# Project stage of an adaptive-layernorm transformer block: token normalisation moved from VectorE to ScalarE, and two of eight subtractions of a half moved to GpSimd

## The reference, cut to what matters

```python
h = _layernorm(x, axis=-1) * (1 + ca) + sa          # (x - m) / sqrt(v + eps), then modulation
x = x + ga * attention(h)
h = _layernorm(x, axis=-1) * (1 + cb) + sb
x = x + gb * ffn(h)

# attention(x):
q = x @ W_q; k = x @ W_k; v = x @ W_v
latent_kv = (k + v) @ W_down_kv
k_rec = latent_kv @ W_up_k; v_rec = latent_kv @ W_up_v
scores = (q k_rec^T / sqrt(256)) * exp(-0.01 * |t - t'|)
out = softmax(scores) @ v_rec @ W_o
```

## Time and profile before

| what | value |
|---|---|
| median of 3 runs | 2593.89 us (2593.72 to 2594.16) |
| the profiled execution | 2596.16 us, of which the span of the trace is 2594.4 us |
| project stage, from the first projections to the last low part | about 36 to 341 us of the span |
| busy over the whole span | PE 93%, VectorE 80%, ScalarE 71%, GpSimd 50% |

### The profile page before, as it was taken

How to read it: one execution, slowest core, us unless ns; L and a number is a source line. 1 busy time by engine, 2 the same in 40 slices (tenths; PEclk the granted TensorE clock), 3 DMA queues, 4 the chain that set the end, 5 groups by cost and what they waited for, 6 DMA issues and landing times. The chain is left out here.

```text
span 2594.4 us, 41397 instructions
## 1 busy us (share of the span) xinstructions
PE 2425.1 (93%) x12710; PEld 1050.6 (40%) x12710; DVE 2068.6 (80%) x3812; ACT 1840.0 (71%) x4200; POOL 1289.9 (50%) x1107
## 2 busy tenths in 40 slices
PE   5878859999999999999999999999986999999998
PEld 2434312333333333333333333333223666666665
DVE  5888878888888888888888888888755878888885
ACT  3666615888888888888888888888843555555553
POOL 3666642534435344353453534534214777777774
PEclk9676757999999999999999999999976999999999
DMA  4777894755756657566574665755302111221110
GB/s 142 240 253 254 247 193 119 155 127 124 158 101 147 135 118 152 113 140 143 112 158 114 140 143 108 155 118 124 80 25 67 57 57 57 57 56 57 54 43 19
DMA packets 273773, 315.58 MB, mean 122 GB/s; under 512 B 38032, under 2 KB 182160, under 8 KB 273424
## 3 DMA queue, kind: packets, MB, share of 16 engines
q1 hardware_dynamic: 264336, 304.54, 49.2%
q10 hardware_dynamic: 9216, 8.39, 0.9%
HBM read 225.78 MB, written 85.46 MB: 120 GB/s over the span
## 5 line engine op out<-in xcount | busy, mean ns | idle before, releaser
L942 DVE CUSTOM_DVE_ANT_0 unread<-max_ps,toeplitz_sb 128x1024 bf16<-128x1024 f32 x1024 | 1215.7, 1222 | 248.9 <-PE max_ps L759 246.6
L871 ACT ACTIVATE probs<-score_ps 128x512 f32<-128x512 f32 (+3 forms) x2560 | 1015.3, 484 | 150.0 <-PE score_ps L788 75.5
L759 PE MATMUL max_ps<-k_low,q_low 96*128 96x512 bf16 x2048 | 718.0, 392 | 27.6 <-DVE ident_bf L933 17.9
L714 POOL TENSOR_TENSOR diag<-diag,diag_decay 128x512 f32<-128x512 f32 x240 | 305.5, 1273 | 811.7 <-ACT diag L880 807.2
L814 PE MATMUL pv_ps<-probs,v 128*32 128x512 f32 x4096 | 545.3, 605 | 1.7 <-ACT probs L900 0.7
L783 PE MATMUL score_ps<-q_up,k_up 99*128 99x512 bf16 (+3 forms) x1280 | 407.6, 319 | 13.9 <-ACT probs L871 12.4
L788 PE MATMUL score_ps<-q_low,k_low 99*128 99x512 bf16 (+3 forms) x1280 | 403.3, 317 | 3.6 <-ACT probs L871 3.0
L726 POOL TENSOR_TENSOR diag<-diag,shift 128x512 f32<-128x512 f32 x256 | 333.8, 1304 | 81.6 <-DVE diag L966 62.4
L1366 PE MATMUL gu_ps<-wgu_t,turned 128*128 128x512 f32 (+1 forms) x768 | 316.7, 562 | 0.8 <-DVE hid L1581 0.8
L759 PEld LDWEIGHTS max_ps<-k_low,q_low 96*128 96x128 bf16 x2048 | 197.0, 98 | 217.7 <-DVE row_max L942 107.5
L783 PEld LDWEIGHTS score_ps<-q_up,k_up 99*128 99x128 bf16 x1280 | 123.5, 97 | 378.3 <-ACT probs L871 201.4
(11 more groups left out here) (154 smaller groups left out, 2853.6 us busy)
## 6 DMA issues: line engine op xcount, KB each, us to landing
shift<-max_whole_dram SPq DMA_DIRECT2D x64, 1024.0 KB, 7.9
splits<-parts SPq DMA_DIRECT2D x128, 384.0 KB, 2.7
q_low<-splits SPq DMA_DIRECT2D x192, 128.0 KB, 7.3
k_low<-splits SPq DMA_DIRECT2D x192, 128.0 KB, 8.6
q_up<-splits SPq DMA_DIRECT2D x192, 128.0 KB, 11.6
k_up<-splits SPq DMA_DIRECT2D x192, 128.0 KB, 12.7
v_padded<-v_out SPq DMA_DIRECT2D x64, 256.0 KB, 3.7
v<-v_padded SPq DMA_DIRECT2D x32, 512.0 KB, 14.9
```

The source lines that it names most:

```text
L714: nc.gpsimd.tensor_tensor(diag[:, g % 2], diag[:, g % 2], diag_decay[:].unsqueeze(1).broadcast_to([P, UH, P]), ALU.mult).then_inc(diag_dec ...
L759: mm = pe.matmul(max_ps[:, i % 2, half * HALF:(half + 1) * HALF], low[0][u][0:KROWS, h, qb * P:(qb + 1) * P], low[1][u][0:KROWS, h, half * ...
L871: op = nc.scalar.activation(probs[:, g % PROBS, h, first:end], score_ps[:, at % RING, first:end], ACT.Exp)
L942: nc.vector.tensor_tensor_reduce(unread[:, i % 2, :], max_ps[:, i % 2, :], toeplitz[:, at:at + S], 1.0, -3.0e38, ALU.mult, ALU.max, row_ma ...
```

## The change

Normalisation goes to ScalarE as one scaled and shifted copy, x * rstd + (-mean * rstd). For that VectorE computes `minus_mean` (128x4) after `var_eps`, and GpSimd computes `offset` = `minus_mean` * `rstd` (128x4) after `rstd`. `var_ready` counts both VectorE operations, `rstd_ready` is now given by the `offset` product, and the power gives a new semaphore, `inverse_ready`, on which the product waits. `normalise(h + 1)` stands at the head of half h in ScalarE's program. VectorE no longer frees `x_in` (`x_free` is gone); SP waits for `xhat_ready` instead. Its place in SP's order is the same.

Of the eight subtractions `rest = full - high` of a half, those of blocks 0 and 4 go to GpSimd, each directly ahead of the low part of the same block; six stay on VectorE. The middle parts of blocks 0 and 4 (ScalarE) wait for GpSimd's new semaphore `pool_rest_ready`, and so does VectorE before it overwrites `full` 0 and 4 a half later.

```diff
+    POOL_RESTS = (0, 4)
         def load_x(b, hf):
             h = 2 * b + hf
-            sp.wait_ge(x_free, h + 1)
+            if h >= 2:
+                sp.wait_ge(xhat_ready, TH * (h - 1))
...
         def statistics(b, hf):
+            if h > 0:
+                dve.wait_ge(rstd_ready, h)
             for i in range(TH):
                 nc.vector.bn_aggr(mean_var[:, i, :], stats[:, i, :]).then_inc(aggr_done, 1)
             dve.wait_ge(aggr_done, TH * (h + 1))
             nc.vector.tensor_scalar(var_eps[:], mean_var[:, :, 1], EPS, None, ALU.add).then_inc(var_ready, 1)
-        def normalise(b, hf):
-            h = 2 * b + hf
-            dve.wait_ge(rstd_ready, h + 1)
-            for i in range(TH):
-                op = nc.vector.tensor_scalar(xhat[hf][:, i, :], x_in[hf][:, i, :], mean_var[:, i, 0:1],
-                                             rstd[:, i:i + 1], ALU.subtract, ALU.mult)
-                op.then_inc(xhat_ready, 1)
-            dve.wait_ge(xhat_ready, TH * (h + 1))
-            dve.sem_inc(x_free, 1)
+            nc.vector.tensor_scalar(minus_mean[:], mean_var[:, :, 0], -1.0, None, ALU.mult).then_inc(var_ready, 1)
...
             def scaled(n):
+                if n in POOL_RESTS and h > 0:
+                    dve.wait_ge(pool_rest_ready, len(POOL_RESTS) * (h - 1) + POOL_RESTS.index(n) + 1)
...
-                if n > 0:
+                if n > 0 and n - 1 not in POOL_RESTS:
                     without_high(n - 1)
...
         def inverse_std(h):
-            pool.wait_ge(var_ready, h + 1)
-            nc.gpsimd.tensor_tensor(rstd[:], var_eps[:], minus_half[:], ALU.pow).then_inc(rstd_ready, 1)
+            pool.wait_ge(var_ready, 2 * (h + 1))
+            if h > 0:
+                pool.wait_ge(xhat_ready, TH * h)
+            nc.gpsimd.tensor_tensor(rstd[:], var_eps[:], minus_half[:], ALU.pow).then_inc(inverse_ready, 1)
+            pool.wait_ge(inverse_ready, h + 1)
+            nc.gpsimd.tensor_tensor(offset[:], minus_mean[:], rstd[:], ALU.mult).then_inc(rstd_ready, 1)
 
         def low_parts(b, hf):
             for n in range(BLOCKS):
                 nb = BLOCKS * (2 * b + hf) + n
-                pool.wait_ge(rest_ready, nb + 1)
+                if n in POOL_RESTS:
+                    pool.wait_ge(high_ready, nb + 1)
+                    nc.gpsimd.tensor_tensor(rest[:, n % RING, :], full[:, n % RING, :], parts[:, n % RING, 0, :],
+                                            ALU.subtract).then_inc(pool_rest_ready, 1)
                 pool.wait_ge(middle_ready, nb + 1)
...
+        def normalise(b, hf):
+            h = 2 * b + hf
+            act.wait_ge(rstd_ready, h + 1)
+            for i in range(TH):
+                nc.scalar.activation(xhat[hf][:, i, :], x_in[hf][:, i, :], ACT.Identity, bias=offset[:, i:i + 1],
+                                     scale=rstd[:, i:i + 1]).then_inc(xhat_ready, 1)
...
         def middle(b, hf, n):
-            act.wait_ge(rest_ready, BLOCKS * (2 * b + hf) + n + 1)
+            h = 2 * b + hf
+            if n in POOL_RESTS:
+                act.wait_ge(pool_rest_ready, len(POOL_RESTS) * h + POOL_RESTS.index(n) + 1)
+            else:
+                others = [i for i in range(BLOCKS) if i not in POOL_RESTS]
+                act.wait_ge(rest_ready, len(others) * h + others.index(n) + 1)
```

More of the change, by code:

```diff
@@ L175, in project_stage @@
     rstd = sb("rstd", [P, TH], F32)
+    minus_mean = sb("minus_mean", [P, TH], F32)
+    offset = sb("offset", [P, TH], F32)
     h_t = [sb(f"h_t{i}", [P, DC, HALF], F32) for i in range(2)]
@@ L198, in project_stage @@
         sem("full_ready"), sem("high_ready"), sem("rest_ready"), sem("middle_ready"), sem("low_ready"))
-    x_free, lat_free, q_free, k_free = sem("x_free"), sem("lat_free"), sem("q_free"), sem("k_free")
+    lat_free, q_free, k_free = sem("lat_free"), sem("q_free"), sem("k_free")
+    inverse_ready, pool_rest_ready = sem("inverse_ready"), sem("pool_rest_ready")
     parts_free = [sem(f"parts_free{i}") for i in range(RING)]
@@ L258, in _ @@
     def _(dve):
-        dve.sem_inc(x_free, 2)
         dve.sem_inc(q_free, 1)
@@ L317, in steps @@
             for hf in range(2):
-                if later(b, hf, 1):
-                    normalise(*later(b, hf, 1))
                 splits(b, hf)
         statistics(0, 0)
-        normalise(0, 0)
         statistics(0, 1)
@@ L466, in steps @@
             for hf in range(2):
+                if later(b, hf, 1):
+                    normalise(*later(b, hf, 1))
                 for n in range(BLOCKS + 1):
@@ L477, in steps @@
                         copy_v(b, hf)
+        normalise(0, 0)
         modulate(0, 0)
```

## The result

The changed kernel takes 2612.83 us (median of 4 runs) against 2593.8 us for the kernel before: a ratio of 1.0075, 95% interval 1.0062 to 1.0087. It is slower by 19 us. The forecast was 2609.4 us, with a range of 2597 to 2626, and a chance of 0.81 of being slower. The profiled execution has a span of 2610.3 us, 15.9 more than before.

What follows compares the result with a forecast made beforehand. A loop through SP's order and the load of x was taken as the bound: 13 halves +13.9, start +1.0, half 0 +0.8, half 14 -0.6, half 15 +0.4, together +15.5 on 2593.89, giving 2609.4 us (range 2597 to 2626).

Steps and rivals of the forecast that it cites:

- The bound: Project stage: a loop from low parts through v stores, load of x, statistics and block 4 sets the half, not VectorE.
- the sum of 19.11: Half 13 before the change, five pieces of the loop: 3.54 + 5.78 + 2.10 + 2.08 + 5.61 us.
- the second path: From the front of the half through PE and ScalarE's second v copy to middle 4; nearly as long as the loop.
- The series behind the variance: Power, offset product, subtraction 4 and middle 4 in series before low 4: 3.58 us instead of 2.08, +1.50.
- the bound of 1.01: Upper bound for the offset product on GpSimd, from the power on the same 128x4; 0.22 us was forecast.
- The upper bound of 1.61: Longest low part, taken as upper bound for subtraction 4 on GpSimd; 1.15 us was forecast.
- Low parts 4 to 7: GpSimd's last four low parts of a half: 5.45 us instead of 5.61, bounds 4.9 and 5.8.
- rival 2: Price hidden: low parts 4 to 7 take 4.9, x lands 0.5 sooner; 2595 to 2598 us, chance 0.10.
- Landing of x: From issue of the load to the statistics: median landing 5.4 us plus 0.1, 5.50 in the loop.
- 20.17: Forecast length of a half in us: 3.54 + 5.50 + 2.10 + 3.58 + 5.45, or +1.07 a half.
- Rival 3: Faster, VectorE the bound after all, if x lands within 3.6 us of its issue: 2584.4 us, chance 0.09.
- the front: From the last low part of one half to the first of the next: 3.2 us instead of 3.83.

Runs made afterwards that it cites:

- the early load: Load of x issued half a half earlier, behind the store of block 4: the changed kernel then takes 2584.76 us, the kernel before 2591.17 us.
- the late load: Load of x left in its place behind the v stores, as in the kernel before (2593.8 us) and the changed kernel (2612.83 us).
- the fastest kernel: Changed kernel with no subtraction moved to GpSimd and the load of x issued half a half earlier: 2570.69 us, 0.9908 of the kernel before.

## Why the prediction was right

**The bound.** The forecast read from the 0.86 us of idle time ahead of the statistics, and from the sum of 19.11, that a loop through SP's order and the load of x sets the half, and not VectorE. For the changed kernel this holds in all of the halves 1 to 13, and the early load takes 2.13 us a half off it. For the kernel before it holds in only 4 of the 13. In the other nine, half 13 among them, high 5 was released by the second v copy; where the k matmuls took 3.78 us, low 4 then started 13.5 us after the half began, whether x was early or late. The sum of 19.11 closes in any case, because its pieces follow each other in time; it does not tell which of two paths came last. In half 13 the two lay within 0.08 us (from the end of `var_eps` to low 4 took 2.08, and 2.00 in halves where the loop decided), so nothing was lost by taking it for the loop. That the second path was the longer one in most halves is why the early load gives the kernel before no more than 0.47 a half.

**The series behind the variance.** Forecast +1.50, measured +1.72 in half 13. The product was 0.20 (0.22 forecast; the bound of 1.01 from the power was not needed). The forecast's own slope and intercept give 0.27 for four columns, not 0.22, so that this term came out so close is luck. `minus_mean` and the start of the power cost 0.15 after the end of `var_eps`, 0.16 forecast. The subtraction was the term that was mis-sized: 1.67 to 1.69 for 1.15 in 12 of the 14 halves that load. Smaller steps took part of that back: from the start of the power to the subtraction 1.23 for 1.38, and from its end to low 4 0.74 for 0.89. The forecast let VectorE read only PSUM at that time, but the subtraction of block 5, which before waited behind block 4's, now starts when high 5 is done, 0.03 us ahead of GpSimd's in the half shown. The upper bound of 1.61 was nearer. The Trainium skill (SBUF — State Buffer, SBUF: two separate sides) has GpSimd and a VectorE operation with two SBUF inputs exclude each other for a whole instruction. The trace agrees in the main: a full wait for VectorE's 0.69 would give 1.81 (1.15 + 0.69 - 0.03), an estimate, and 1.68 was measured. In half 3, where GpSimd's subtraction began 0.04 us ahead of VectorE's, it took 1.15 and VectorE's took 1.67.

**Low parts 4 to 7.** 5.45 forecast, 5.39 measured; nothing came of the 4.9 that rival 2 needed.

**Landing of x.** 5.50 forecast, 5.25 in half 13, a median landing of 5.2 for 5.4. This fell on the other side by what the subtraction had too much, so that 20.17 and 20.16 agree better than their terms, and that is luck. Rival 3 asked for a landing within 3.6 us; the shortest was 3.9, of the load for half 2, which is issued before the loop runs, and in the loop the shortest was 4.4. One sign that the forecast named did not come: VectorE was to stand idle some 2 us or more ahead of the statistics in every half, and in the halves 1 to 13 it stood idle 1.19 to 2.39 us, in 11 of them under 2.

**ScalarE.** Four copies in 2.06 us, 2.0 forecast, at no cost; the front came to 2.99 us (299.51 to 302.50) for 3.2 forecast, with 1.09 to the start of subtraction 0. (For that start the forecast's sum has 1.2, though its own text puts high 0 some 1.4 after low 7.) Half 14 took 18.08 where 18.93 less 0.6 was forecast.

**The rest of the sum.** Half 0 ended 1.37 later for 1.8 forecast. The last two halves are off by 1.9 - (-0.2) = 2.1 us in the first profile and scatter by as much. Later stages gave 1.2 us back in the first profile (17.1 in the stage, 15.9 in the span), which was not looked into. The median differs by 19.0, the first pair of profiled executions by 15.9 (2612.1 against 2596.16), and the change's four runs lie between 2609.61 and 2617.19, so the forecast of +15.5 is as near as the runs allow one to say.

## What to carry to other kernels

When a stage repeats, measure the distance of one event from period to period, and write the period as a closed sum of pieces before asking which engine is busiest: here an engine at 86% did not set the period, and relieving it by way of GpSimd made the kernel slower. Such a sum closes along any path, so look in every period, and not in one, at what released the instruction where two paths meet. Work moved to an idle engine is paid where it stands in that engine's order and by which path is the longer one there: with the late load subtraction 0 was free and subtraction 4 cost 1.6 us a half, behind a wait for late data; where the path from the front decides, subtraction 0 cost 0.5 and subtraction 4 only 0.3. And where the loop closes through a transfer that is only late because of its place in the queue's order, moving that one instruction was worth more here than any work moved between engines, and it turned the sign of a change made beside it.

## What the runs showed of the hardware that was not expected

In the fastest kernel the halves alternate between 16.5 and 17.6 us: 16.52, 17.57, 16.52, 17.56 and so on. PE's granted clock alternates with them (0.79 and 0.71 of 2.4 GHz in the two windows above), and the four matmuls for k, on the path from the front, fall now at the full clock and now at 1.2 GHz. The timeline of PE shows them in half 12 and in half 13:

```profile
247.46 1.98 PE L398 MATMUL k_ps<-lat_t,wup_k_sb 64*128 64x512 f32 x4 [1.30 <-ACT lat_t L451]
```

```profile
263.98 3.78 PE L398 MATMUL k_ps<-lat_t,wup_k_sb 64*128 64x512 f32 x4 [1.29 <-ACT lat_t L451]
```

In the changed kernel they took 3.77 or 3.78 us in every half but the first, so there is no such difference there. It accounts for what the fastest kernel was below its expectation: the 17.6 was read from a half with k matmuls of 3.78 us, the long halves do take 17.56, and with the short ones the mean is 17.08.
